# A derived second normalisation, a new order of VectorE's list, and 70 steps without a loop

## The reference

```python
x2 = layernorm(x1) @ sum(factors) / sqrt(8) + bias + x1
x3 = lightning_attention(layernorm(x2)) @ Wo + x2 # 16 heads, chunks of 128, state carried on
n  = layernorm(x3)                                # (x3 - mean) / sqrt(var + eps)
r  = x3 + n                                       # residual that is stored
xf = layernorm(n) * gamma + beta                  # normalised a second time
# xf chooses for each token one of 64 tiles by the signs of xf, and 8 elements of it
# are replaced by a spline value that is added to r
```

## Time and profile before

| | |
|---|---|
| runs (3): median, lowest, highest | 5924.46, 5921.22, 5928.32 us |
| the profiled execution's own time | 5923.98 us |
| its span, first to last instruction | 5922.2 us |
| TensorE, VectorE, GpSimd, ScalarE busy in the span | 86%, 83%, 55%, 44% |
| mean granted clock of TensorE | 0.937 |

### The profile page before, as it was taken

The page is one execution under the profiler, slowest core; times in us unless marked ns, Lnnn a source line. Parts: engine busy times, 40 slices in busy tenths (PEclk is TensorE's granted clock), DMA queues, the critical chain, the costliest instruction groups (busy, mean ns, idle before and its releaser), DMA issues. The chain is left out here.

```text
span 5922.2 us, 110904 instructions
## 1 busy us (share of the span) xinstructions
PE 5088.3 (86%) x41157; PEld 3047.7 (51%) x41157; DVE 4925.7 (83%) x7468; ACT 2610.0 (44%) x4180; POOL 3231.1 (55%) x1675
## 2 busy tenths in 40 slices
PE   6899999999999999999999998668888888888822
PEld 3444444444444444444444444246666777777722
DVE  3888988888888889889888888568888888888888
ACT  3655655655556556556556555212222222222200
POOL 1676676676766766766766767423333333333323
PEclk9999999999999999999999999879999998899855
DMA  2221222222222222212222222220000000000034
GB/s 84 76 101 65 100 99 74 94 87 79 101 81 85 101 79 86 95 72 101 90 76 101 85 81 94 91 86 25 20 22 22 20 23 20 24 20 20 18 111 138
DMA packets 139954, 421.27 MB, mean 71 GB/s; under 512 B 38368, under 2 KB 39904, under 8 KB 106592
## 3 DMA queue, kind: packets, MB, share of 16 engines
q1 hardware_dynamic: 136672, 411.75, 19.8%
q10 hardware_dynamic: 2816, 3.51, 0.2%
HBM read 361.99 MB, written 53.22 MB: 70 GB/s over the span
## 5 line engine op out<-in xcount | busy, mean ns | idle before, releaser
L335 POOL TENSOR_TENSOR s<-s,Cb 128x1024 f32<-128x1024 f32 x1024 | 2393.7, 2359 | 1083.8 <-DVE state L656 1073.0
L651 DVE TENSOR_TENSOR_SCAN s<-s,state,BU 128x512 f32<-128x512 f32 x2048 | 2452.7, 1260 | 425.4 <-PE BU L737 391.5
L501 ACT ACTIVATE s<-dt,ch 128x512 f32<-128x512 f32 x2048 | 1305.6, 712 | 778.6 <-PE Y L754 777.1
L754 PE MATMUL Y<-s,ident 64*64 64x512 f32 x8192 | 1011.8, 609 | 76.2 <-POOL s L335 75.3
L683 PE MATMUL PJ<-xnT,w_in 128*128 128x512 f32 x2048 | 946.9, 606 | 9.1 <-ACT dtuT L367 5.7
L737 PEld LDWEIGHTS BU<-spread,dtuT 32*128 32x128 f32 x16384 | 512.7, 189 | 528.4 <-DVE s L651 403.0
L737 PE MATMUL BU<-spread,dtuT 32*128 32x128 f32 x16384 | 611.2, 286 | 145.5 <-DVE s L651 140.8
L683 PEld LDWEIGHTS PJ<-xnT,w_in 128*128 128x128 f32 x2048 | 370.1, 190 | 479.0 <-issue 424.2
L754 PEld LDWEIGHTS Y<-s,ident 64*64 64x64 f32 x8192 | 279.3, 134 | 571.5 <-issue 533.8
L728 PE MATMUL PJ<-w_out,u 128*128 128x512 f32 x1024 | 472.8, 606 | 8.2 <-ACT xnT L371 6.7
L1110 POOL TENSOR_TENSOR x1t<-x1t,bias_b 128x512 f32<-128x512 f32 x64 | 81.1, 1267 | 525.8 <-DVE xa L1282 525.8
(11 more groups left out here) (218 smaller groups left out, 7634.8 us busy)
## 6 DMA issues: line engine op xcount, KB each, us to landing
Cb<-bc SPq DMA_DIRECT2D x256, 1024.0 KB, 4.9
res<-in_x SPq DMA_DIRECT2D x64, 256.0 KB, 4.9
x<-res SPq DMA_DIRECT2D x64, 256.0 KB, 5.2
x1t<-x SPq DMA_DIRECT2D x64, 256.0 KB, 2.6
out<-r_t SPq DMA_DIRECT2D x64, 256.0 KB, 2.0
xt<-in_x SPq DMA_DIRECT2D x31, 512.0 KB, 5.5
x_all<-out SPq DMA_DIRECT2D x16, 512.0 KB, 4.2
scm<-out SPq DMA_DIRECT2D x16, 512.0 KB, 4.6
```

The costliest lines, as they stand in the source:

```text
L335: nc.gpsimd.tensor_tensor(pair, pair, Cb[q % 2][:, 2 * part * T:2 * part * T + 2 * T], ALU.mult).then_inc(z_ready, 1)
L501: nc.scalar.activation(s[k % SLOTS][:, n, :], dt[p % 2][:, gi, :], ACT.Exp, scale=ch[:, 2 * p + gi, 7 + 4 * nq + n:8 + 4 * nq + n]).then_i ...
L651: nc.vector.tensor_tensor_scan(s[k % SLOTS][:, n, :], s[k % SLOTS][:, n, :], BU[:, n::4], state[:, b, k, n:n + 1], ALU.mult, ALU.add).then ...
L754: last_ = nc.tensor.matmul(Y[r][y_rows(r, gi), :], ident[rows, rows], s[(k_even + gi) % SLOTS][rows, n, :], start=False, stop=(n == 3 and ...
```

## The change

Three things are changed in the second stage.

`x3n` is no longer made. From the statistics of `x3` and the first reciprocal `rd` VectorE works out the variance of the second normalisation (`var * rd * rd`), and a scale `1 + rd` and shift `-mean * rd`. ScalarE makes `r_t` as `x3 * scale + shift` in one activation; GpSimd's addition is gone. `xf` is computed straight from `x3` with the product of both reciprocals, `rd_cd`.

The order of VectorE's and ScalarE's lists changes. VectorE's is now: low parts, `qdT`, statistics a and c, `xa`, `x2` with statistics b, the small operations of tile t-5, `xb`, the scores, `xf`, `scm`, rotary step, `x3`, `kvu`. ScalarE makes the roots a, c, b, d and `r_t` together ahead of its copies of q, k and v.

The loop in `steps` is gone: all 70 steps are written out on every engine.

```diff
--- before.py
+++ after.py
@@ -954,7 +954,8 @@
         rrms = [sb(f"rrms{i}", [P, 1]) for i in range(2)]
         aTs = [sb(f"aTs{i}", [P, KB, P], F32R) for i in range(2)]
         x3 = [sb(f"x3_{i}", [P, HID]) for i in range(2)]
-        x3n = [sb(f"x3n{i}", [P, HID]) for i in range(2)]
+        r_scale = [sb(f"r_scale{i}", [P, 2]) for i in range(2)]
+        rd_cd = sb("rd_cd", [P, 1])
         r_t = [sb(f"r_t{i}", [P, HID]) for i in range(2)]
         xf = [sb(f"xf{i}", [P, HID]) for i in range(2)]
         sg = [sb(f"sg{i}", [P, HID], BF16) for i in range(2)]
@@ -1020,7 +1021,7 @@
         high_ready = {n: sem(f"high_ready_{n}") for n in ("xT", "x2T", "aT")}
         names = ("w_loaded2", "part_loaded0", "part_loaded1", "part_used", "setup_dve", "setup_act", "setup_pool", "setup_pe",
                  "xa_ready", "x1b_ready", "x2_ready", "xb_ready", "rot_parts", "qk_ready", "kd_ready", "qd_ready",
-                 "kvd_ready", "kvu_ready", "kv_ready", "rms_ready", "x3_ready", "x3n_ready", "r_ready",
+                 "kvd_ready", "kvu_ready", "kv_ready", "rms_ready", "x3_ready", "scale_ready", "r_ready",
                  "xf_normed", "xf_scaled", "xf_ready", "sg_ready", "ohx_ready", "scored")
         S = {n: sem(n) for n in names}
         sp_steps, qt_copied, pe_steps = sem("sp_steps2"), sem("qt_copied"), sem("pe_steps2")
@@ -1036,12 +1037,7 @@
 
         def steps(eng, body):
 
-            for t in range(8):
-                body((None, t))
-            with eng.Fori(2, TILES // 4) as i:
-                for u_ in range(4):
-                    body((i, u_))
-            for t in range(TILES, TILES + LAST_STAGE):
+            for t in range(TILES + LAST_STAGE):
                 body((None, t))
 
         @block.sync
@@ -1094,14 +1090,6 @@
             pool.wait_ge(S["setup_act"], 1)
 
             def body(t):
-                a = back(t, 5)
-                if valid(a):
-                    s_ = a[1] % 2
-
-                    wait(pool, S["x3n_ready"], num(a) + 1)
-                    if a[0] is not None or a[1] >= 2:
-                        pool.wait_ge(r_stored[s_], 16 * stored_count(a))
-                    nc.gpsimd.tensor_tensor(r_t[s_][:], x3[s_][:], x3n[s_][:], ALU.add).then_inc(S["r_ready"], 1)
                 a = t
                 if valid(a):
 
@@ -1181,8 +1169,6 @@
                     a = back(t, 2)
                     wait(act, filled["v"], num(a))
                     take_high("x2T", a, xbT)
-                if valid(back(t, 5)):
-                    root("c", back(t, 5), 5)
                 if valid(back(t, 4)):
                     a = back(t, 4)
                     s_ = a[1] % 2
@@ -1200,7 +1186,18 @@
                 if valid(t):
                     root("a", t, 0)
                 if valid(back(t, 5)):
-                    root("d", back(t, 5), 5)
+                    root("c", back(t, 5), 5)
+                if valid(back(t, 1)):
+                    root("b", back(t, 1), 1)
+                if valid(back(t, 5)):
+                    a = back(t, 5)
+                    s_ = a[1] % 2
+                    root("d", a, 5)
+                    wait(act, S["scale_ready"], num(a) + 1)
+                    if a[0] is not None or a[1] >= 2:
+                        act.wait_ge(r_stored[s_], 16 * stored_count(a))
+                    nc.scalar.activation(r_t[s_][:], x3[s_][:], ACT.Identity, bias=r_scale[s_][:, 1:2],
+                                         scale=r_scale[s_][:, 0:1]).then_inc(S["r_ready"], 1)
                 if valid(back(t, 2)):
                     a = back(t, 2)
                     s_ = a[1] % 2
@@ -1211,8 +1208,6 @@
                     take("k", a, qk[s_][:, 1, :])
                     wait(act, filled["at"], num(a) - 1)
                     take("v", a, vv[s_][:])
-                if valid(back(t, 1)):
-                    root("b", back(t, 1), 1)
                 if valid(back(t, 5)):
                     a = back(t, 5)
                     wait(act, S["xf_ready"], num(a) + 1)
@@ -1346,8 +1341,6 @@
                 s5, s3, s2, s1, s4 = back(t, 5), back(t, 3), back(t, 2), back(t, 1), back(t, 4)
                 if valid(s1):
                     low("xT", s1, xaT)
-                if valid(s5):
-                    stats("c", x3[s5[1] % 2][:])
                 if valid(s2):
                     low("x2T", s2, xbT)
                 if valid(s4):
@@ -1363,19 +1356,11 @@
                     dve.wait_ge(x1_loaded[t[1] % 2], 16 * (stored_count(t) + 1))
                     stats("a", x1t[t[1] % 2][:])
                 if valid(s5):
-                    s_ = s5[1] % 2
-                    wait(dve, S["r_ready"], num(s5) - 1)
-                    norm("c", s5, x3[s_][:], x3n[s_][:], S["x3n_ready"])
-                    dve.drain()
-                    stats("d", x3n[s_][:])
-                if valid(back(t, 6)):
-                    score(back(t, 6))
+                    stats("c", x3[s5[1] % 2][:])
                 if valid(t):
 
                     wait(dve, filled["xT"], num(t) - 1)
                     norm("a", t, x1t[t[1] % 2][:], xa[t[1] % 2][:], S["xa_ready"])
-                if valid(s5):
-                    norm("d", s5, x3n[s5[1] % 2][:], xf[s5[1] % 2][:], S["xf_normed"])
                 if valid(s1):
 
                     dve.wait_ge(filled["ffn"], num(s1) + 1)
@@ -1386,6 +1371,39 @@
                     nc.vector.bn_stats(ln["b"][0][:], x2[s1[1] % 4][:]).then_inc(S["x2_ready"], 1)
                     dve.drain()
                     nc.vector.bn_aggr(ln["b"][1][:], ln["b"][0][:]).then_inc(var_ready["b"], 1)
+                if valid(s5):
+                    s_ = s5[1] % 2
+                    mean, var, rd = ln["c"][1][:, 0:1], ln["c"][1][:, 1:2], ln["c"][3][:]
+                    dve.wait_ge(sd_ready["c"], num(s5) + 1)
+                    wait(dve, S["r_ready"], num(s5) - 1)
+                    nc.vector.reciprocal(rd, ln["c"][2][:])
+                    dve.drain()
+                    nc.vector.tensor_scalar(ln["d"][1][:, 1:2], var, rd, rd, ALU.mult, ALU.mult
+                                            ).then_inc(var_ready["d"], 1)
+                    nc.vector.tensor_scalar_add(r_scale[s_][:, 0:1], rd, 1.0)
+                    nc.vector.tensor_scalar(r_scale[s_][:, 1:2], mean, rd, -1.0, ALU.mult, ALU.mult)
+                    dve.drain().then_inc(S["scale_ready"], 1)
+                if valid(s1):
+                    wait(dve, filled["x2T"], num(s1) - 1)
+                    norm("b", s1, x2[s1[1] % 4][:], xb[s1[1] % 2][:], S["xb_ready"])
+                if valid(back(t, 6)):
+                    score(back(t, 6))
+                if valid(s5):
+                    dve.wait_ge(sd_ready["d"], num(s5) + 1)
+                    nc.vector.reciprocal(ln["d"][3][:], ln["d"][2][:])
+                    dve.drain()
+                    nc.vector.tensor_tensor(rd_cd[:], ln["c"][3][:], ln["d"][3][:], ALU.mult)
+                    dve.drain()
+                    nc.vector.tensor_scalar(xf[s5[1] % 2][:], x3[s5[1] % 2][:], ln["c"][1][:, 0:1], rd_cd[:],
+                                            ALU.subtract, ALU.mult).then_inc(S["xf_normed"], 1)
+                if valid(s3):
+
+                    wait(dve, filled["at"], num(s3))
+                    for r in range(4):
+                        dve.wait_ge(filled[f"sc{r}"], num(s3) + 1)
+                        nc.vector.tensor_tensor(scm[:, r, :, :].rearrange("p k n -> p (k n)"), bank(f"sc{r}")[:],
+                                                decay[:, r, :, :].rearrange("p k n -> p (k n)"), ALU.mult
+                                                ).then_inc(taken[f"sc{r}"], 1)
                 if valid(s2):
                     s_ = s2[1] % 2
                     dve.wait_ge(taken["k"], num(s2) + 1)
@@ -1400,17 +1418,6 @@
                             rs_[:, :, z, :], pairs[:, :, 1 - z, :],
                             sin[:, z, :].unsqueeze(1).to_broadcast([P, 2 * HEADS, ROT]), ALU.mult)
                     dve.drain().then_inc(S["rot_parts"], 1)
-                if valid(s1):
-                    wait(dve, filled["x2T"], num(s1) - 1)
-                    norm("b", s1, x2[s1[1] % 4][:], xb[s1[1] % 2][:], S["xb_ready"])
-                if valid(s3):
-
-                    wait(dve, filled["at"], num(s3))
-                    for r in range(4):
-                        dve.wait_ge(filled[f"sc{r}"], num(s3) + 1)
-                        nc.vector.tensor_tensor(scm[:, r, :, :].rearrange("p k n -> p (k n)"), bank(f"sc{r}")[:],
-                                                decay[:, r, :, :].rearrange("p k n -> p (k n)"), ALU.mult
-                                                ).then_inc(taken[f"sc{r}"], 1)
                 if valid(s4):
                     s_ = s4[1] % 2
                     dve.wait_ge(S["rms_ready"], num(s4) + 1)
```

## The result

| | before | changed |
|---|---|---|
| runs: median, lowest, highest | 5924.22 (4), 5921.22, 5928.32 | 5604.01 (4), 5602.68, 5612.12 us |
| profiled execution, its span | 5923.98, 5922.2 | 5612.12, 5610.2 us |
| mean granted clock | 0.937 | 0.957 |

The ratio is 0.9464 [0.9453, 0.9475]: 320 us less. The forecast was 5630, with 5600 to 5685 as its range, so the result lies 4 us above the low end.

A forecast was written before the change was run, and what follows sets the result against it. VectorE's own list was taken as the bound, with TensorE waiting inside it. Terms cut 26.53 us a step to 21.99, 22.3 with straight code's 0.3; 293.5 us off 5923.98 gave 5630 us, range 5600 to 5685.

The forecast's parts named there:

- part 1: VectorE, second stage: x3n and its statistics out (1.50 us), small operations in (0.68); net -0.82 us a step.
- `r_t` on ScalarE: r_t moves from GpSimd to ScalarE, ahead of the q, k and v copies: cost 0, or 1.5 us without cover.
- `xf`: VectorE's xf, placed after the scores with nothing queued on GpSimd, falls from 1.47 to 0.55: -0.92 us a step.
- `xb`: VectorE's xb, placed between small operations and scores, falls from 1.23 to 0.55: -0.68 us a step.
- Rotary step after `scm`: On VectorE, rc takes 0.96 instead of 1.64: -0.68 us; GpSimd's later addition stays hidden with 0.4 us to spare.
- The gap: VectorE's wait ahead of xaT goes, as 3.7 us of work behind scm covers the 3.29 return path: -1.44 us.
- `x2` earlier: Takes away TensorE's 2.70 us wait ahead of wo; pays only by keeping TensorE off the path.
- Written out: Second-stage loop replaced by straight code: 0.71 us a step goes, 0.3 comes in; about 24 us of the gain.
- TensorE becomes the bound: TensorE's round of 21.2 us grows to 22.65 at clock 0.94; 22.7 a step, 5654 us; chance 0.20.
- Straight code stalls as much as the loop: Written-out second stage costs 0.71 us a step instead of 0.3: 22.7 a step, 5654 us; chance 0.12.
- GpSimd still blocks: GpSimd goes on holding VectorE's xf, xb and rc: 2.28 us stay, 24.6 a step, 5764 us; chance 0.06.
- Fetching eats it: Instruction fetch stalls in 70 written-out bodies: three a step eat the whole 5.2 us gain; chance 0.04.

The follow-up runs named there:

- The best version: Changed kernel with reciprocal rrms moved between scm and rc, and the drain ahead of scale_ready left out: 5577.95 us, ratio 0.9420 to the kernel before.

## Why the prediction was right, point by point

The mechanism held in each part: TensorE waited inside VectorE's list, the list got shorter, and TensorE stayed under it. The sum was 0.2 us a step too long and the price of straight code 0.16 too high, together 0.38 us a step, 22 us over 58 steps: nearly all of the distance to 5604. That the sum came so close is in part luck: part 1 gave 0.20 us a step less than its term, and `pr`, which had no term, gave 0.28 more, so that the two errors nearly cancel.

1. *Derived statistics.* The prediction's net of -0.82 was mis-sized. What comes in is 0.88 us, not 0.68: `rd_c` to `rd_b` takes 0.88 (4524.64 to 4525.52) in place of one reciprocal with its drain, 0.24, and one product with its drain, 0.24, stands ahead of `xf`. 1.50 out and 0.88 in is -0.62; the two runs on the new order that differ only in this part and in who makes `r_t` are 41 us apart, 0.66 a step. The best version shows that 0.27 of the 0.88 was one drain.
2. *`r_t` on ScalarE.* Cost 0 was right, with 0.82 us on an idle engine. The copy of q waits until 4526.13 and nobody waits for it. But the part had a gain that the prediction didn't see: the timeline of before had `pr` at 0.70 us, and I took that for its length. In the kernel before GpSimd added `r_t` just then, and `pr` (4536.67 in the earlier trace rows) ends 0.29 us after it:

```profile
4535.79 1.29 POOL L1104 TENSOR_TENSOR r_t<-x,x3n 128x512 f32<-128x512 f32 x1 [5.00 <-DVE x3n L1282]
```

`pr` takes 0.40 to 0.43 in every run in which that addition is gone or moved, and 0.69 to 0.81 in the kernel before: -0.28 in this step.
3. *`xf`*, 4. *`xb`.* -0.92 and -0.68, as forecast, in 58 of 58 steps (mean 547 ns each):

```profile
L1277 DVE TENSOR_SCALAR xb<-x_all,mv_b,rd_b 128x512 f32<-128x512 f32 x58 | 31.7, 547 | 4.9 <-issue 0.4
L1397 DVE TENSOR_SCALAR xf<-x,mv_c,rd_cd 128x512 f32<-128x512 f32 x58 | 31.7, 547 | 4.9 <-issue 0.4
```

5. *Rotary step after `scm`.* Forecast 0.96, measured 0.95. The prediction had GpSimd's lateness hidden by 0.4 us; TensorE shows no wait for it. What this place is worth shows in the run that undid it: nearly the whole gain.
6. *The gap.* -1.44 as forecast. The margin is thin, as said: with 0.15 us less behind `scm`, ScalarE's high part is seen again ahead of `xaT`.
7. *`x2` earlier.* TensorE's wait of 2.70 is gone and the granted clock is 1.00. The prediction booked that as worth nothing by itself. The run with the rotary step ahead of `scm` shows what it may protect: after 41 of 58 waits of 3.2 to 4.3 us TensorE came back slow, at a granted clock of 0.61 in the window shown. In the kernel before the two waits of 2.7 us left the step of the earlier trace rows at 1.00, and no run moves `x2` alone, so what this part is worth by itself stays open.
8. *Written out.* The 0.71 went, and straight code costs 0.14 us a step here and 0.21 in the old order, not 0.3: a stall of 0.35 to 0.4 in about every third step. The Trainium skill, Runtime: NRT & Kernel Launch, section "Instruction fetch mechanics", calls the crossing of a block in straight code mostly hidden, and a taken branch to a page that is not at hand a stall; the runs fit both, at 0.14 us a step and at 3.3 us an edge, and mostly hidden is not the cost of 0 that the prediction read there. That these stalls are fetches is argued from that, not shown. The sentence "about 24 us of the gain come from writing out" was wrong for the new order: it is 60 there, and 34 on the old. The 0.71 was taken from edges that hid 1.44 us of their stall under the return path. Once part 6 removed that wait, the loop would have cost 1.13 us a step (1328.13 / 58 - 21.77). The sum was untouched by this, because both are gone in the end.

Adding up the measured terms: 26.53 - 0.62 - 0.92 - 0.68 - 0.69 - 1.44 - 0.28 = 21.90, and the plain step is 21.77. The 0.13 that is left is spread over short entries and I have not traced it.

Of the rivals, "TensorE becomes the bound" fails on its waits for `scm`, 0.6 us in the mean of 57 steps, and the clock that it needed (0.94) is 1.00. "Straight code stalls as much as the loop" fails by 0.14 against 0.71. "GpSimd still blocks" fails on the three entries; its mechanism was real, and three of the runs above bring it back (`rd_cd`, `rs`, `xb`). "Fetching eats it" would have needed three stalls of 1.9 us in each step; there is one of 0.4 in three.

## What to carry to other kernels

When one engine's list is the bound, look for entries that are longer than the same operation elsewhere in the trace, and read what the other engine on the same memory was doing at their end: four entries here (`xf`, `xb`, `rc`, `pr`) were held, and reordering freed 2.6 us of a 26.5 us step without removing any work. Order the list also so that the work behind the last hand-over covers the return path, and count each drain as a small operation. Price the removal of a loop edge after the other edits, not before: a stall that lay under another wait comes out in full once that wait is gone.

## What the runs showed of the hardware

- A VectorE product of 128x1 with two inputs took 1.23 us instead of 0.16 beside a GpSimd addition of 128x512 (`rd_cd`). The Trainium skill, SBUF — State Buffer, section "SBUF: two separate sides", has the lock on the shared ports held for a whole instruction; the trace agrees, and shows that an instruction as small as this one waits too.
- It goes for bf16 inputs too: `pr`, 0.42 us alone and 0.69 to 0.81 beside GpSimd's addition. `scm`, which reads PSUM, and the statistics, which read one tensor, kept 2.48 and 0.69 us beside GpSimd instructions.
- GpSimd pays as well: its gamma product took 1.67 us instead of 1.28 where it started 0.16 us after `rc` (rotary step ahead of `scm`).
- GpSimd took 0.77 us for 512 columns from one tensor and 1.28 from two.
- In the two windows shown TensorE had stood idle for 3.2 us, the next 5 to 7 us ran at a granted clock of 0.54 to 0.61, that is mostly at 1.2 GHz, and the stretch after that at 0.96 to 1.00. It is not so each time: 17 of the 58 waits of 3.2 to 4.3 us in the run with the rotary step ahead of `scm` were followed by a turn of q and k at full speed (1.07 us; slow turns take 1.95), one of them in a window of 7 us at 1.00 (4329.00 to 4336.00).
